# One group of attention matmuls moved ahead of one projection chunk, in the order of four engines

## The reference, cut to what matters

```python
q = (x @ Wq).reshape(b, s, 64, 64); k = ...; v = ...      # 128 -> 4096 each
q = relu(q) * SCALE;  k = relu(k)
kv  = einsum('bsid,bsjd->bsdj', k, v)
out = einsum('bsid,bsdj->bsij', q, kv)
q_norm = einsum('bsid,bsd->bsi', q, k.sum(axis=2))
out = (out / (q_norm[..., None] + EPS)).reshape(b, s, 4096) @ Wo + bo
x = layernorm(x + out)
h = silu(fp4_linear(x, w_gate)) * fp4_linear(x, w_up)      # 128 -> 352
x = layernorm(x + fp4_linear(h, w_down))                   # 352 -> 128
```

## Time and profile before

| | us |
|---|---|
| median of 3 runs | 2271.65 |
| the profiled execution, whole | 2271.46 |
| its span, first to last instruction | 2269.7 |
| PE busy in the span | 2050.3 (90%) |
| DVE busy | 1805.8 (80%) |
| POOL busy | 1690.7 (74%) |
| ACT busy | 1618.7 (71%) |

### The profile page before, as it was taken

The page is one execution under the profiler, slowest core; times in us unless marked ns, Lnnn a source line. Parts: engine busy times, 40 slices in busy tenths (PEclk is TensorE's granted clock), DMA queues, the critical chain, the costliest instruction groups (busy, mean ns, idle before and its releaser), DMA issues.

```text
span 2269.7 us, 88816 instructions
## 1 busy us (share of the span) xinstructions
PE 2050.3 (90%) x37963; PEld 1961.0 (86%) x37963; DVE 1805.8 (80%) x3359; ACT 1618.7 (71%) x3210; POOL 1690.7 (74%) x2192
## 2 busy tenths in 40 slices
PE   4799999999999999999999999999999999999975
PEld 3788998898898898898899899899899889889874
DVE  6778888888888888888888887888888888888873
ACT  4667777777777777777777777777777777777761
POOL 4577787787787787787787778778778778778772
PEclk9999999999999999999999999999999999999996
DMA  6467656666656666756756766765765665665661
GB/s 194 95 133 151 139 127 146 141 130 142 148 125 139 147 132 134 156 126 133 159 124 134 153 132 129 155 133 127 152 137 127 148 141 127 143 146 126 139 130 33
DMA packets 523216, 308.32 MB, mean 136 GB/s; under 512 B 275590, under 2 KB 497734, under 8 KB 522310
## 3 DMA queue, kind: packets, MB, share of 16 engines
q1 hardware_dynamic: 522822, 302.65, 61.9%
HBM read 17.38 MB, written 4.19 MB: 10 GB/s over the span
## 4 chain that ended last, share of the span: by engine, by line
PE 55%; POOL 18%; issue 9%; ACT 9%; DVE 6%; DMA 2%; SPq 0%; DVEq 0%; ACTq 0%; POOLq 0%
PE ps L408 15%; PE ps L361 12%; PE ps L363 12%; PE ps L362 12%; POOL o_st L1078 8%; POOL q_nat L1068 7%; ACT q_bd L564 6%; DVE q L798 3%; PE ps L434 3%; DVE o L816 2%; ACT hqT L571 2%; POOL small L1086 2%; PE ps L445 1%; DMA x_in<-in_L_attn_x 1%; ACT ks L577 1%
## 5 line engine op out<-in xcount | busy, mean ns | idle before, releaser
L1078 POOL TENSOR_TENSOR o_st<-o,o_st 128x256 bf16<-128x256 f32 x1024 | 659.8, 679 | 5.9 <-ACT o_st L639 5.9
L1068 POOL TENSOR_TENSOR q_nat<-q,q_nat 128x512 bf16<-128x512 f32 x512 | 590.3, 1176 | 33.2 <-ACT q_nat L597 32.9
L639 ACT CAST o_st<-o 128x256 bf16<-128x256 f32 x1024 | 358.4, 403 | 214.8 <-DVE o L816 211.0
L361 PE MATMUL ps<-v_st,q_bd 128*128 128x66 bf16 x4096 | 456.3, 198 | 42.9 <-DVE o L816 37.5
L361 PEld LDWEIGHTS ps<-v_st,q_bd 128*128 128x128 bf16 x4096 | 419.7, 114 | 61.9 <-DVE o L816 56.3
L362 PE MATMUL ps<-v_st,q_bd 128*128 128x66 bf16 x4096 | 454.0, 198 | 0.0
L363 PE MATMUL ps<-v_st,q_bd 128*128 128x66 bf16 x4096 | 452.5, 197 | 0.0
L816 DVE TENSOR_TENSOR o<-ps,rec 128x512 f32<-128x512 f32 x512 | 344.5, 683 | 120.7 <-POOL o_st L1078 110.2
L362 PEld LDWEIGHTS ps<-v_st,q_bd 128*128 128x128 bf16 x4096 | 417.5, 116 | 0.2 <-issue 0.2
L363 PEld LDWEIGHTS ps<-v_st,q_bd 128*128 128x128 bf16 x4096 | 416.8, 115 | 0.0
L408 PE MATMUL ps<-w_o,o_st 128*128 128x128 bf16 x6144 | 376.9, 220 | 3.4 <-DMA o_st<-swap 3.4
(11 more groups left out here) (129 smaller groups left out, 5334.4 us busy)
## 6 DMA issues: line engine op xcount, KB each, us to landing
q_bd<-q_nat SPq DMA_DIRECT2D x256, 256.0 KB, 3.9
swap<-v_st SPq DMA_DIRECT2D x64, 576.0 KB, 5.1
v_st<-v_st SPq DMA_DIRECT2D x64, 576.0 KB, 5.6
v_st<-swap SPq DMA_DIRECT2D x64, 576.0 KB, 5.4
swap<-o_st SPq DMA_DIRECT2D x64, 512.0 KB, 4.9
o_st<-o_st SPq DMA_DIRECT2D x64, 512.0 KB, 6.8
o_st<-swap SPq DMA_DIRECT2D x64, 512.0 KB, 5.5
x_in<-in_L_attn_x SPq DMA_DIRECT2D x64, 64.0 KB, 5.3
```

The costliest lines, as they stand in the source:

```text
L361: nc.tensor.matmul(dst, lhs(0), rhs(0), start=True, stop=False)
L639: last = nc.scalar.copy(ost[1 - t.par][:, 0, :, a, g * G:(g + 1) * G, :], src[:, a])
L1068: last = nc.gpsimd.tensor_tensor(qnat[:, 1, a, :, e, :], src[:, a], qnat[:, 0, a, :, e, :], ALU.subtract)
L1078: last = nc.gpsimd.tensor_tensor(lo[:, :, a], src[:, a], hi[:, :, a], ALU.subtract)
```

## The change

On TensorE `out_group(t, 0)` goes ahead of `project(t, "q", 0)`. On ScalarE `x1_keep` goes ahead of `k_sums`, and `o_hi(t, 0)` from behind `sigmoid` to ahead of `norm_o(t, 1)`. On VectorE `scale_o(t, 0)` goes right behind `recip(t, 0, 1)`. On GpSimd `o_lo(t, 0)` goes ahead of `rstd_2` and `q_lo(t, 0)`. Nothing is added or taken away, and the slot table stays.

```diff
@@ TensorE
                 down(t)
+                out_group(t, 0)
                 project(t, "q", 0)
-                out_group(t, 0)
                 k_sum(t)
                 out_group(t, 1)
@@ ScalarE
                 q_stay(t, 0, 0)
                 norm_o(t, 0)
+                x1_keep(t)
                 k_sums(t)
                 if t.is_(1):
                     down_weights()
-                x1_keep(t)
+                o_hi(t, 0)
                 norm_o(t, 1)
                 xq_copy(t)
                 q_hi(t, 0)
                 sigmoid(t)
-                o_hi(t, 0)
                 o_hi(t, 1)
@@ VectorE
                 recip(t, 0, 1)
+                scale_o(t, 0)
                 stats_2(t)
                 q_scale(t, 0)
                 before_mean_2(t)
                 mean_2(t)
                 recip(t, 1, 1)
-                scale_o(t, 0)
                 scale_o(t, 1)
@@ GpSimd
                 x_back(t)
+                o_lo(t, 0)
                 rstd_2(t)
                 q_lo(t, 0)
-                o_lo(t, 0)
                 o_lo(t, 1)
```

## The result

The changed kernel takes 2336.48 us, the median of 4 runs (2332.54 to 2338.29), against 2272.19 of the kernel before in 4 runs: a ratio of 1.0279, with a 95% interval of 1.0267 to 1.0292. It is slower, as forecast, but by 64 us where 39 were forecast, and outside the range of 2295 to 2326. The profiled execution took 2335.13 us with a span of 2333.3. The mean granted clock of the four runs is 0.972 to 0.975, against 0.980 to 0.986 in the runs of the kernel before.

A forecast was written before the change was run, and what follows sets the result against it. TensorE's own work plus its waits was taken to bound each turn. Out 0's new wait (+1.02), `h_scale` (-0.05) and out 5 (-0.33) gave 0.64 us; 60 turns plus 1.0 made 39.4, so 2311 us, range 2295 to 2326.

The forecast's parts named there:

- the clock: Rival on TensorE: two waits around one short product drop the clock to 1.2 GHz; 2430 us, chance 0.01.
- the sum: Forecast total: 60 full turns at 0.64 us plus 1.0 make 39.4 us, added to 2271.5.
- The new wait: TensorE, out 0 waits 1.15 us for ScalarE's third copy into `q_bd`; the sum of k starts 1.02 us later.
- `o_hi(0)` in gate's way: ScalarE, `o_hi(0)` ahead of `xq_copy`: taken as 0 delay to gate, 0 to 0.3 us kept for the range.
- `h_scale`: VectorE, held until a GpSimd piece ends, which comes some 0.1 us sooner relatively: 0.05 off, out 4 at +0.97 us.
- Out 5's 0.33 given back: TensorE, out 5 no longer delayed by GpSimd's `o_lo(1)`: follows out 4 after 0.82 us instead of 1.15, at +0.64.
- The rest of the turn: After out 5: nothing new; v0 of the next turn loses 0.3 of its 0.40 us room behind `scale_o(6)`.
- Turns 1 to 3: First turns: 0 in turns 1 and 2, 1.0 us in turn 3; bounds 0 to 4 us together.
- the mechanism that was forecast as the likeliest: Full turns: out 0's new wait, less what out 5 gives back, costs 0.64 us each; 2311 us, chance 0.75.
- nothing given back: Rival: late GpSimd and VectorE cause waits at out 5, out 6 or v0; 1.02 stays, 2333 us, chance 0.09.

The follow-up runs named there:

- the second experiment: Changed kernel with TensorE's q0 back ahead of out 0, leaving only the ScalarE, VectorE and GpSimd parts: 2297.0 us, ratio 1.0110 to the kernel before.
- the last experiment: The whole change on the kernel before with third copy a turn ahead, `hq_copy` ahead of the second, k folded first: 2260.12 us, ratio 0.9952.
- the run with k's sum waiting: Kernel before with ScalarE's third `q_bd` copy a turn ahead and `hq_copy` ahead of the second copy: 2246.58 us, ratio 0.9888.

## Why the prediction was wrong

The step that failed is the clock, a term that the sum put at nothing: it cost some 21 of the 64 us. The wait that was forecast is there at its size. The terms one by one:

**The new wait: right.** Out 0 was to start at 1.92 us behind the down product and does at 1.93; the sum of k was to come at +1.02 and does.

**`o_hi(0)` in gate's way, 0: right for this change.** Gate comes at 5.99 against 5.01, and its wait is 34.2 us against 33.4. Where TensorE's part is missing the term is 0.6 us, as the second experiment shows.

**`h_scale`: right in kind, small in size.** It takes 0.52 us in turn 31 instead of 0.64: GpSimd's piece ends at 1131.22 (1130.58 + 0.64) and `h_scale` at 1131.29, so it ends behind a piece again, and that piece ends sooner relative to it. Gate comes 0.98 late and out 4 0.86. The sum had 0.97 for out 4, with 0.05 for this term; it gave 0.12.

**Out 5's 0.33 given back: right.** It no longer waits; the Wo product behind it comes 0.51 late (1133.85 - 1120.29 = 13.56 against 13.05), so 0.35 was given back.

**The rest of the turn, 0: mis-sized, 0.18.** I had looked at v0 and let 0.3 of its room of 0.40 go. In fact all of the room goes and 0.10 more:

```profile
1141.40 0.69 DVE L816 TENSOR_TENSOR o<-ps,rec 128x512 f32<-128x512 f32 x1 [0.40 <-POOL o_st L1078]
```

`scale_o(6)` waits 0.40 us for GpSimd and ends at 1142.09, that is 21.80 behind the down product instead of 20.94, and v0 starts 0.15 behind that. The last Wo matmul had started at 1142.08, so 0.16 lies between two starts where 0.056 would do; no row of waits shows it. Another 0.08 is lost at v3, whose slot is v0's and which waits for VectorE behind ScalarE's first `v_hi`; that one is late because `o_hi(7)` is. So a turn is 0.69 longer where 0.64 stood. That these are so close is partly luck: 0.13 too little had been taken off at out 4 and out 5, and 0.18 was missing behind them.

**The clock: this is the step that failed.** The sum had no term for it, and as a rival it had a chance of 0.01, on the strength of one window in which TensorE idled for 2.64 us and the clock stayed up. That row shows one wait passing once. It doesn't show that two, 0.77 us of work apart, pass 60 times, and it was an exception itself. The same wait, ahead of v0 of turn 2, stands in every kernel here (2.64 to 2.66 us), and in nine of the eleven profiles, the changed kernel's among them, the clock falls within it or within 1.0 us behind it; only the kernel before and the one with the old wait filled (from turn 4 on, so not here) got past. V0 to v3 of turn 2 in the kernel before (first line) and in the changed one (second):

```profile
99.90:105.28 5.38, 5.38 (x96) 5.36 (x97) 3.21 (x4) 4.24 (x7) 5.21 (x8) 1.00 0.72 153
98.78:105.76 6.98, 6.98 (x97) 6.98 (x97) 3.24 (x4) 4.34 (x7) 6.81 (x8) 0.76 0.78 167
```

The Trainium skill's warning (TensorE: Matmul & The Clock Gate, "HAM oscillation — how this bites in real kernels") was the right one to weigh and I set it aside; its case is longer waits than any in the full turns here, and the measurements go beyond it. The size was off as well: I priced a fall in every turn at 2 us; it comes in 11 of 59 and costs 1.6. Which turns it hits is open: the distances between them are near even (4 to 6 turns here, 2 to 4 with TensorE's part alone), and no run tells why.

The account of the two spans, 2333.3 - 2269.7 = 63.6 us: 59 turn lengths at 0.69 make 40.7; 11 falls at 1.6 make 17.6; the time up to the first down product 3.0 (180.88 against 177.92); the last turns 1.7; small scatter 0.6. Turns 1 to 3 were put at 1.0, within bounds of 0 to 4. But the 3.0 holds two more falls, the one just shown and one at 147.3 us, behind a single wait of 2.72 us ahead of out 0 of turn 3, at 1.6 each. So what the order costs there can't be told from nothing, and the clock has some 21 of the 64 us.

So the mechanism that was forecast as the likeliest happened, with some 42 of the 64 us belonging to it, and the clock came on top; none of the cases combined the two. With either wait filled the kernel takes 2319 us, which is inside the range. That the measured 2336 lies by the 2333 of "nothing given back" is chance: out 5's wait was given back.

## What to carry to other kernels

Before a product is moved ahead, look at what ran in its old place: here q0 was the cover of a copy 1.9 us long, and no wait showed it because it was hidden. And put a price on TensorE's idle time itself: a new wait beside an old one can bring the clock down although each passes alone. A row in which the clock stayed up once is one draw, not a rule: here the next kernels fell at the same place. When a wait is the problem, ask which instruction of the engine that is waited for could run at another time: here one copy a turn earlier and two orders changed gave 1.8%, where moving TensorE's own work cost 2.8%.

## What the runs showed of the hardware

- Two waits of TensorE of about 1.0 us, with a product of 0.77 us between them, brought the granted clock from 2.4 to 1.2 GHz in 11 of 59 rounds, and 1.6 us were lost each time. With either of the two filled by matmuls it happened in none.
- It happened in none of the full turns of the kernel without the third copy, nor with waits of 0.54 and 1.17 us with 3.8 us of work between them in the last experiment, nor with 1.08 and 1.17 us and 4.5 us between them in the second. Once it happened in the run with k's sum waiting (one turn of 34.89 us among 33.33).
- The wait of 2.64 to 2.66 us ahead of v0 of turn 2, with waits of 0.9 us and less shortly before it, brought the granted clock down in nine of eleven profiles. Behind a single wait of 2.72 us ahead of out 0 it fell in turn 3 of the changed kernel (147.3 us) and not in turn 2.
- Matmuls whose result is thrown away cost nothing in a wait of known length: 1080 of them left the turn at 34.46 us and made the kernel 17.5 us faster.
- A `tensor_scalar` on 22 numbers takes mostly 0.63 to 0.65 us beside GpSimd's work in the kernel before and 0.51 to 0.55 in the changed one, and 0.18 in turn 65, where GpSimd has no group.
